# Decoder layer with an int8 feed-forward on one core: the int8-to-bf16 casts of the up stage go from ScalarE to GpSimd and are issued earlier

## The reference, cut to what matters

```
def _act_fake_quant(x, clip_factor):
    scale = sigmoid(clip_factor) * max(abs(x)) / 127
    return clip(round(x / scale), -128, 127) * scale
...
xq   = _act_fake_quant(layernorm(x), clip_x[0])
gate = einsum('bsh,ih->bsi', xq, _weight_fake_quant(w_gate))   # 704 x 256
up   = einsum('bsh,ih->bsi', xq, _weight_fake_quant(w_up))     # 704 x 256
h    = _act_fake_quant(silu(gate) * up, clip_down[0])
out  = x + einsum('bsi,hi->bsh', h, _weight_fake_quant(w_down))
```

## Time and profile before

| | |
|---|---|
| median of 3 runs | 677.8 us (677.54 to 679.78) |
| the profiled execution | 679.08 us, span 677.3 us |
| TensorE matmul, busy in the span | 624.2 us (92%) |
| VectorE | 513.4 us (76%) |
| ScalarE | 403.6 us (60%) |
| GpSimd | 166.8 us (25%) |

### The profile page before, as it was taken

How to read it: one execution, slowest core, us unless ns; L and a number is a source line. 1 busy time by engine, 2 the same in 40 slices (tenths; PEclk the granted TensorE clock), 3 DMA queues, 4 the chain that set the end, 5 groups by cost and what they waited for, 6 DMA issues and landing times.

```text
span 677.3 us, 20152 instructions
## 1 busy us (share of the span) xinstructions
PE 624.2 (92%) x8105; PEld 398.5 (59%) x8105; DVE 513.4 (76%) x984; ACT 403.6 (60%) x601; POOL 166.8 (25%) x215
## 2 busy tenths in 40 slices
PE   2989999999999999999999998999998979888885
PEld 2647565767765676566667665566755745333364
DVE  6688866878787667566875885677768778689897
ACT  3336666675675557576545566446354683899692
POOL 2005332431343210240152013123102011344300
PEclk9989999999999999999999999999997999999999
DMA  7644133462434243437334353434257240000024
GB/s 257 184 143 160 34 117 111 149 173 61 119 105 118 86 135 87 121 107 174 110 74 114 114 137 85 117 80 128 71 133 218 67 85 1 1 0 1 1 93 156
DMA packets 58266, 71.61 MB, mean 106 GB/s; under 512 B 23819, under 2 KB 35263, under 8 KB 58175
## 3 DMA queue, kind: packets, MB, share of 16 engines
q1 hardware_dynamic: 54495, 68.36, 36.0%
q10 hardware_dynamic: 3680, 1.97, 1.1%
HBM read 17.21 MB, written 4.69 MB: 32 GB/s over the span
## 4 chain that ended last, share of the span: by engine, by line
PE 64%; DVE 14%; SPq 6%; issue 5%; ACT 5%; DMA 4%; ACTq 0%; DVEq 0%
PE banks L493 42%; PE banks L680 7%; PE banks L600 4%; PE banks L691 4%; SPq L426 3%; DVE mtop L1148 3%; PE banks L543 2%; DVE tops L1360 2%; SPq L421 2%; SPq L444 1%; ACT xnT L1024 1%; DVE big L1353 1%; PE banks L759 1%; PE banks L603 1%; DVE oTs L1398 1%
## 5 line engine op out<-in xcount | busy, mean ns | idle before, releaser
L493 PE MATMUL banks<-big 96*128 96x77 bf16 (+3 forms) x1348 | 161.3, 241 | 6.7 <-DVE mtop L1152 2.0
L1148 DVE TENSOR_REDUCE mtop<-banks 128x4 f32<-128x640 f32 (+3 forms) x128 | 127.4, 1020 | 39.3 <-PE banks L609 38.9
L493 PEld LDWEIGHTS banks<-big 99*128 99x128 bf16 (+2 forms) x1348 | 104.3, 103 | 73.9 <-issue 31.5
L1459 POOL TENSOR_SCALAR_AFFINE_SELECT big<-big 128x512 f32<-128x512 f32 x96 | 65.5, 682 | 229.9 <-ACT big L939 229.1
L939 ACT ACTIVATE big<-banks 128x1024 f32<-128x1024 f32 x96 | 97.1, 1030 | 40.3 <-PE banks L493 40.0
L493 PE MATMUL banks<-xnT,weights 128*128 128x512 f32 x192 | 93.6, 617 | 0.2 <-DVE mtop L1148 0.2
L600 PE MATMUL banks<-big 96*32 96x160 bf16 (+3 forms) x1792 | 69.6, 253 | 1.3 <-DVE mtop L1148 0.9
L943 ACT ACTIVATE big<-banks 77x1024 f32<-77x1024 f32 x48 | 47.8, 1022 | 27.9 <-PE banks L493 26.1
L1152 DVE TENSOR_REDUCE mtop<-banks 128x8 f32<-128x616 f32 x64 | 49.4, 791 | 16.8 <-PE banks L493 16.5
L680 PE MATMUL banks<-big 128*17 128x256 f32 x768 | 57.0, 382 | 0.0
L952 ACT COPY oe<-banks 128x512 f32<-128x512 f32 x64 | 36.9, 590 | 30.2 <-DMA oTx<-oe 9.9
(11 more groups left out here) (171 smaller groups left out, 1213.2 us busy)
## 6 DMA issues: line engine op xcount, KB each, us to landing
big<-parts SPq DMA_DIRECT2D x285, 128.0 KB, 2.5
oc<-sums SPq DMA_DIRECT2D x15, 512.0 KB, 4.8
oTs<-oe SPq DMA_DIRECT2D x64, 64.0 KB, 2.4
out_dram<-oTs SPq DMA_DIRECT2D x16, 256.0 KB, 2.2
xs<-in_x_dram SPq DMA_DIRECT2D x3, 1024.0 KB, 5.5
big<-oe SPq DMA_DIRECT2D x32, 64.0 KB, 2.3
oTx<-oe SPq DMA_DIRECT2D x32, 64.0 KB, 2.3
xs<-in_x_dram SPq DMA_DIRECT2D x2, 512.0 KB, 6.4
```

Of the source, the lines that this page charges most:

```text
L493: return e.matmul(to[0:w], k[:, 0:w], q, start=start, stop=stop, skip_group_check=True)
L1148: e.tensor_reduce(M.rearrange("p (h c) -> p h c", h=4)[:, :, c], pair(p).rearrange("p j (s n) -> p (j s) n", s=2)[:, :, 0:160 + 32 * (c % 4)],
L1459: e.affine_select(out=P[:, :, 0:128], in_=P[:, :, 0:128], compare_op=ALU.is_ge, fill=0.0, base=0, pattern=[[0, 4], [1, 128]], channel_mult ...
```

## The change

GpSimd does the casts in place of ScalarE. Each moves up in the list: the cast for block 1 stays at tile 0 of block 0, and the cast for block b + 2 now stands behind `keepx` of tile 4 in block b, where the cast for block b + 1 stood at tile 0 of block b. In GpSimd's queue it thus lies between hid 3 and hid 5, a block earlier than it is needed. Its waits are the same.

```
@@ the order
                 ffn.append(("up", blk, t))
-                if blk < 7 and t in (0, 2, 4):
-                    ffn.append(({0: "castx", 2: "turnx", 4: "keepx"}[t], blk + 1))
+                if (blk, t) == (0, 0):
+                    ffn.append(("castx", 1))
+                if blk < 7 and t in (2, 4):
+                    ffn.append(({2: "turnx", 4: "keepx"}[t], blk + 1))
+                if blk < 6 and t == 4:
+                    ffn.append(("castx", blk + 2))
                 if blk < 6 and t == 1:
                     ffn += [("narrow", blk + 2, c) for c in range(4)]
                 ffn.append(("hid", blk, t))
@@ run_scalar
-                if k == "castx":
-                    blk = s[1]
-                    i = (blk % 2) * 1024
-                    e.wait_ge(f_x8, 4 * blk + 4)
-                    if blk > 1:
-                        e.wait_ge(f_tx, blk)
-                    else:
-                        e.wait_ge(d_scale, len(JOBS) + 1)
-                    e.copy(xb[:, i:i + 1024], x8[:, i:i + 1024]).then_inc(f_xb, 1)
-                elif k == "keepx":
+                if k == "keepx":
@@ run_gpsimd
             for s in ffn:
                 k = s[0]
-                if k == "hid" and by_pool(s):
+                if k == "castx":
+                    blk = s[1]
+                    i = (blk % 2) * 1024
+                    e.wait_ge(f_x8, 4 * blk + 4)
+                    if blk > 1:
+                        e.wait_ge(f_tx, blk)
+                    else:
+                        e.wait_ge(d_scale, len(JOBS) + 1)
+                    e.tensor_copy(xb[:, i:i + 1024], x8[:, i:i + 1024]).then_inc(f_xb, 1)
+                elif k == "hid" and by_pool(s):
```

## The result

The changed kernel takes 687.99 us (median of 6 runs, 686.61 to 692.12); the kernel before, in six runs of the same collection, 678.71 us (677.14 to 680.65). The ratio is 1.0114, with a 95% interval of 1.0082 to 1.0146: slower, as forecast, but by 9.3 us instead of the forecast 4.8, and the time lies above the range, which ended at 686.

The account below looks back on a forecast made before the run. The prediction took a ring of waits through VectorE, TensorE and ScalarE as the bound. Block 0: 0, block 1: +1.5, blocks 2 to 5: +3.8, block 6: -0.5 made +4.8 on 677.8, so 682.6 us; range 677.2 to 686.

Parts of the forecast that it names:

- The ring bounds a block, and the cast is not on it: Up stage: waits through VectorE, TensorE and ScalarE set each block's 7.37 to 7.40 us; removing ScalarE's cast there gains 0.
- the collision: Up stage: GpSimd's product for tile 1 runs during VectorE's four narrow operations, costing 0.95 us in a block.
- Hid 1 moves forward into the narrows: GpSimd's product for tile 1, today 0.1 us after VectorE's four narrow operations, would be asked for in their middle.
- T: Start of ScalarE's silu of tile 0 in each up-stage block; the forecast cuts blocks and gives times from it.
- The int8 narrow is shut out, for 0.95 us on the ring: One VectorE narrow waits out GpSimd's operation, lengthening the block's chain of waits by 0.95 us.
- In each of blocks 1 to 5: The meeting of GpSimd's tile 1 product with VectorE's narrows was to repeat in all five blocks, 0.95 us each.
- some blocks only: Rival: the meeting happens in some up-stage blocks, as the order of starts tips by 0.1 us; 679 to 681 us, chance 0.05.
- Block 6 gives 0.5 back: Up stage, block 6, without narrow work: the cast is on the path, so removing it brings -0.5 us.
- Block 0: nothing: Up stage, block 0: time freed before the silu of tile 3 becomes waiting for TensorE; worth 0.
- Block 1: 1.5 us: Up stage, block 1: a second queued 2.3 us cast delays hid 5, so two narrows are held, 0.55 + 0.95 us.
- The bound from below, 1.27: Lower price bound for GpSimd's 128x1024 cast, from its affine select of 0.635 us for 512 columns: 1.27 us.
- the estimate of 0.9 us that stood beside it: GpSimd's cast at the skill's best one-input rate, 1.03 cycles a column: 0.9 us, a rate no row shows.

Follow-up runs that it names:

- hid 1 late: The changed kernel with hid of tile 1 issued behind up and hid of tile 2; ratio 1.002 to the kernel before, up stage -0.8 us.
- filler on TensorE: The changed kernel with eight matmuls of constants before up of tile 5 in blocks 1, 2, 3 and 5; ratio 1.0094 to the kernel before; profiled twice.
- engine only: The changed kernel with GpSimd's casts put back at tile 0 of the block before; ratio 1.013 to the kernel before, up stage +8.5 us.

## Why the prediction was right and wrong

- *The ring bounds a block, and the cast is not on it*: right. Without the collision blocks 1 to 5 stay at 7.36 to 7.40 us (hid 1 late).
- *Hid 1 moves forward into the narrows*: right, at T + 1.92 against T + 1.95 in blocks 2 and 5. In blocks 1 and 4 it starts at T + 2.21, because silu 1 waits for TensorE a little, and just meets the fourth narrow. Shown by two kernels that put it back, one by more work on ScalarE, one by the order; both lose the whole collision.
- *The int8 narrow is shut out, for 0.95 us on the ring*: right; 8.32 less 7.37. *In each of blocks 1 to 5*: only as long as the clock is full. In the changed kernel's three profiles one or two of the five escape, each behind a dip; the rival "some blocks only" had this, for another reason.
- *Block 6 gives 0.5 back*: 0.54 in hid 1 late and in both profiles of the filler on TensorE, 0.25 in all three profiles of the changed kernel. There the silu of tile 1 waits for TensorE and starts at T + 0.86; in the others it follows the silu of tile 0 directly, at T + 0.57. That is the 0.29 us between them; what holds TensorE back there stays open. The changed kernel, then the filler on TensorE (T = 633.15 and 631.60):

```profile
634.01 0.69 ACT L1019 ACTIVATE xnT<-banks,winv 128x512 f32<-128x512 f32 x1 [0.17 <-PE banks L759]
```
```profile
631.60 1.27 ACT L1021 ACTIVATE xnT<-banks,winv 128x512 f32<-128x512 f32 x2
```
- *Block 0: nothing*: it gave 0.25 (7.09 against 7.34).
- *Block 1: 1.5 us*: 0.95, for the cast takes 1.04 us and not 2.3. The bound from below, 1.27, was too high as well; the estimate of 0.9 us that stood beside it was the nearest. The special case that block 1 was given did not arise: it costs what blocks 2 to 5 cost.
- *Sum of these*: with the measured terms 5 x 0.95 less 0.54 and 0.25 is +4.0 us, and the filler on TensorE has exactly that. The forecast +4.8 was 0.8 us too high for what it counted (0.55 in block 1, 0.25 in block 0), and this hid part of what it did not count: that the up stage's +5.8 is only 1.0 away is in part luck.
- *Small slips*: the forecast's own range does not follow from its terms: 5 x 0.8 less 0.5 gives 681.3 for its lower end, not 680.8, and 4 x 1.1 + 0.55 + 1.1 less 0.5 gives 683.4 for its upper end, not 683.6. The 0.51 ns a column comes out as 0.52.
- **What failed in the sum: it had no term for TensorE's clock.** It let the ring stretch and priced the stretch at its own length. The wait before up of tile 5 went from 1.04 us to 2.2 to 2.5 us, and at two of these waits in each profile the clock fell to half for 3.4 us. Net of the narrows that escape behind a dip, and with the 0.29 us of block 6, this is 1.8 us (73.76 and 73.77 against 71.95) in two of three profiles, and 0.7 in the third. The bounds of "the remaining 0.66, with its own range of 680.8 to 683.6 (cast bounds, and 0.8 to 1.1 us for a meeting)" took in no dip.
- **What put the time above the range: the base.** The step "the median of the runs is 677.8; I put the sum on the median: 682.6 us" had no width for it. The up stage's +5.8 on 677.8 would be 683.6, still inside. The way from 682.6 to 688.0 is 1.0 us in the up stage, 0.9 because six runs of the kernel before have 678.7, and 3.5 outside the up stage, which in the two profiled executions lie ahead of it. With 23 and 22 runs the kernel before has 680.9 and 681.5, about 3 us above the base that was taken, and the second pair of medians, 681.46 and 687.14, differs by 5.7 us, as the up stages do. So the 3.5 us of the first pair are most likely scatter: the three profiles of the changed kernel have the stage start at 575.2 to 579.7 us, the two of the kernel before at 574.9 and 577.5, in a stretch with the same steps. One profile can't show it, and three runs showed 2.2 us of what is 9 us in 44. What makes that stretch vary stays open, and that the change adds nothing there is not shown either.

## What to carry to other kernels

Work taken off an engine that is busy 97% of the time brought 0.8 us of 6.5 here at best, since a ring through other engines set the pace in most blocks; it can bring a loss, for what stood behind it comes earlier and may meet something that it used to miss by 0.1 us. So ask of each operation set free what else runs at its new time, above all GpSimd beside VectorE's f32 TENSOR_SCALAR from SBUF to SBUF (the reduction, also from SBUF, was not disturbed). A wait that grows on TensorE may be paid twice, once as itself and once in its clock. And ask how far the base of a sum moves from run to run before its range is set.

## What the runs showed of the hardware

- GpSimd's CAST of 128x1024 int8 to bf16 takes 1.04 us, 1.0 ns a column; ScalarE's took 1.05. The copy of 512 permuted f32 columns (1.15 us, 2.2 ns a column) was no guide.
- An int8 output does not keep VectorE's f32 TENSOR_SCALAR out of GpSimd's way: 0.41 us alone, 1.36 us behind a GpSimd TENSOR_TENSOR, 0.15 us past its end; a GpSimd CAST shuts it out as well (1.20 us, engine only). VectorE's reduction beside a GpSimd operation stays at 1.74 us. The Trainium skill, "SBUF — State Buffer", section "Who interferes with whom", has this for tensor_scalar in a two-port mode; the runs agree, and show it for an int8 output.
- TensorE at half clock: two stretches of 3.4 us in each of the three profiles of the changed kernel within the up stage, none in the five profiles whose blocks have waits of 0.85 to 1.45 us at that place, and none that begins in blocks where matmuls of constants filled the wait. All twelve stretches in the table begin from 0.1 us before to 1.2 us after the end of a wait of TensorE of 2.0 to 2.7 us; eight other waits of this length had none behind them.
